# Layer norms of the token tower: five small operations moved to one visit of POOL, with new instruction orders

## What is computed

```
x = embed[tokens] + pos                                     # D = 128
for i in range(2):                                          # the "token tower"
    x = x + scan_attn(ln(x, eps=1e-6))                      # q, k, v; causal convolution of k and v; gates; 8 heads
    x = x + gelu(ln(x, eps=1e-6) @ ff1 + b1) @ ff2 + b2
h = ln(x, eps=1e-6) @ out_k + out_b                         # 256 columns
h = h + linear_attention(layernorm(h, eps=1e-5))            # no softmax, 16 heads of 64
h = h + (silu(n @ wg.T) * (n @ wu.T)) @ wd.T,  n = layernorm(h, eps=1e-5)
```

## Time and profile before

| | us |
|---|---|
| median of 3 runs | 1989.66 |
| lowest, highest | 1988.47, 1992.6 |
| the profiled execution, its own time | 1988.27 |
| its span, first to last instruction | 1986.1 |
| TensorE busy | 1850.2 |
| VectorE, ScalarE, POOL busy | 1165.6, 733.4, 439.4 |
| mean granted clock of TensorE | 0.982 of full speed |

### The profile page before, as it was taken

How to read it: one execution, slowest core, us unless ns; L and a number is a source line. 1 busy time by engine, 2 the same in 40 slices (tenths; PEclk the granted TensorE clock), 3 DMA queues, 4 the chain that set the end, 5 groups by cost and what they waited for, 6 DMA issues and landing times.

```text
span 1986.1 us, 41766 instructions
## 1 busy us (share of the span) xinstructions
PE 1850.2 (93%) x17146; PEld 1588.0 (80%) x17146; DVE 1165.6 (59%) x3019; ACT 733.4 (37%) x1444; POOL 439.4 (22%) x391
## 2 busy tenths in 40 slices
PE   4799999999999999969899999999999999999998
PEld 3678888888888888758688888888888888888887
DVE  2668888888888888755554344434444444444443
ACT  1334444554455555334323322232233223322332
POOL 3233223333222222111121122112211221122112
PEclk8899999999999999989899999999999999999999
DMA  3000000000000000022000000000000000000000
GB/s 94 5 12 18 18 17 18 16 19 16 18 17 16 15 5 9 18 86 80 17 22 1 22 22 22 1 22 22 22 1 22 22 22 1 22 22 22 1 22 22
DMA packets 29211, 42.38 MB, mean 21 GB/s; under 512 B 5856, under 2 KB 22624, under 8 KB 29024
## 3 DMA queue, kind: packets, MB, share of 16 engines
q1 hardware_dynamic: 23648, 33.49, 5.1%
q0 software_dynamic: 2048, 4.20, 0.8%
q10 hardware_dynamic: 3328, 2.04, 0.4%
HBM read 22.93 MB, written 16.78 MB: 20 GB/s over the span
## 4 chain that ended last, share of the span: by engine, by line
PE 73%; DVE 17%; issue 4%; DMA 3%; POOL 2%; ACT 1%; SPq 1%; another core or an unknown queue 0%; DVEq 0%; POOLq 0%; ACTq 0%
PE ps L1406 11%; PE ps L1407 10%; PE ps L1408 10%; PE ps L806 3%; PE ps L1008 3%; PE ps L1456 3%; PE ps L1472 3%; DVE bxn L1271 3%; PE ps L887 3%; PE ps L807 3%; PE ps L808 3%; PE ps L959 3%; PE ps L937 2%; DVE bstats L1255 2%; DMA h<-h_rows 2%
## 5 line engine op out<-in xcount | busy, mean ns | idle before, releaser
L1245 POOL TENSOR_TENSOR hids_low<-hid,hids_high 128x512 fp32r<-128x512 f32 x96 | 137.6, 1440 | 611.0 <-ACT hids_high L1392 611.0
L512 POOL TENSOR_TENSOR rstd<-var,minus_half 128x4 f32<-128x4 f32 x80 | 82.5, 1032 | 564.5 <-DVE var L599 564.4
L757 ACT ACTIVATE xn<-x,shift,rstd 128x128 f32<-128x128 f32 x320 | 130.3, 482 | 133.6 <-DVE shift L604 133.6
L676 DVE TENSOR_TENSOR att<-ps,causal 128x512 f32<-128x512 f32 x256 | 158.6, 681 | 18.1 <-PE ps L937 18.0
L1406 PE MATMUL ps<-r_high,wq_high 128*128 128x256 f32 x512 | 147.4, 288 | 0.7 <-issue 0.7
L1407 PE MATMUL ps<-r_low,wq_high 128*128 128x256 f32 x512 | 144.9, 283 | 0.0
L1408 PE MATMUL ps<-r_high,wq_low 128*128 128x256 f32 x512 | 144.8, 283 | 0.0
L1386 ACT ACTIVATE silu<-ps 128x512 f32<-128x512 f32 x96 | 57.4, 598 | 226.5 <-DVE hid L1321 159.9
L1008 PE MATMUL ps<-w_f,wide 128*128 128x128 f32 x1024 | 130.1, 278 | 0.2 <-ACT wide L801 0.2
L1008 PEld LDWEIGHTS ps<-w_f,wide 128*128 128x128 f32 x1024 | 120.8, 192 | 6.0 <-issue 5.0
L1308 DVE TENSOR_TENSOR m_low<-ps,m_high 128x512 fp32r<-128x512 f32 x32 | 22.1, 692 | 170.8 <-ACT m_high L1378 170.8
(11 more groups left out here) (352 smaller groups left out, 5060.9 us busy)
## 6 DMA issues: line engine op xcount, KB each, us to landing
h_rows<-h_out SPq DMA_DIRECT2D x16, 512.0 KB, 2.8
h<-h_rows SPq DMA_DIRECT2D x16, 512.0 KB, 3.8
out<-bxn SPq DMA_DIRECT2D x32, 256.0 KB, 2.6
taps<-in_filters ACTq DMA_DIRECT2D x1, 1024.0 KB
emb<-in_embed,idx POOLq DMA_INDIRECT x64
wk<-in_W_kT SPq DMA_DIRECT2D x1, 1024.0 KB, 6.6
stage<-in_W_vT SPq DMA_DIRECT2D x2, 512.0 KB, 6.6
stage<-in_W_q SPq DMA_DIRECT2D x2, 512.0 KB, 5.6
```

The lines of the kernel that those rows point to most:

```text
L512: pool.tensor_tensor(rstd[s][:], var[s][:], minus_half[:], ALU.pow)\
L676: dve.tensor_tensor(masked[:, :, PAIR * g:PAIR * g + PAIR, :], bank("qk", s, l, j, g, t)[:].rearrange("p (n r t) -> p n r t", n=2, r=PAIR) ...
L757: act.activation(xn[s][:, j, :], x[s][:, j, :], ACT.Identity, bias=shift[s][:, j:j + 1], scale=rstd[s][:, j:j + 1]).then_inc(xn_made[s].se ...
L1245: pool.tensor_tensor(hids[1][:, halves, :], hid[:, half, :], hids[0][:, halves, :].bitcast(F32), ALU.subtract).then_inc(hid_low[s].sem, 1)
```

## The change

The constant add moves from VectorE's `stats` to POOL, and -mean x `rstd` is done there in two steps: POOL makes `var` and -mean, then the power, then the product, in one visit. The step `shift` is gone, its order entries too. The signals are counted anew: `ln_step` rises by two a norm, `ln_rstd` by four, and `xn` waits for the fourth. The norms of the second half (`b_stats`, `b_pow`) keep their code.

```diff
@@ token_tower
-    ln_step = signals("ln_step", 4 * LN)
-    ln_rstd = signals("ln_rstd", LN)
+    ln_step = signals("ln_step", 2 * LN)
+    ln_rstd = signals("ln_rstd", 4 * LN)
@@ gpsimd
         elif step == "pow":
-            pool.wait_ge(ln_step[s].sem, ln_step[s].at(t, 4 * l + 3))
-            pool.tensor_tensor(rstd[s][:], var[s][:], minus_half[:], ALU.pow)\
-                .then_inc(ln_rstd[s].sem, 1)
+            g = ln_rstd[s]
+            pool.wait_ge(ln_step[s].sem, ln_step[s].at(t, 2 * l + 2))
+            pool.tensor_scalar(var[s][:], mv[s][:, :, 1], EPS_LN, None, ALU.add).then_inc(g.sem, 1)
+            pool.tensor_scalar(shift[s][:], mv[s][:, :, 0], -1.0, None, ALU.mult).then_inc(g.sem, 1)
+            pool.wait_ge(g.sem, g.at(t, 4 * l + 2))
+            pool.tensor_tensor(rstd[s][:], var[s][:], minus_half[:], ALU.pow).then_inc(g.sem, 1)
+            pool.wait_ge(g.sem, g.at(t, 4 * l + 3))
+            pool.tensor_tensor(shift[s][:], shift[s][:], rstd[s][:], ALU.mult).then_inc(g.sem, 1)
@@ vector
-            dve.wait_ge(g.sem, g.at(t, 4 * l + 1))
+            dve.wait_ge(g.sem, g.at(t, 2 * l + 1))
             dve.sem_inc(passed)
             for j in range(J):
                 ins = dve.bn_aggr(mv[s][:, j, :], stats[s][:, j, :])
             ins.then_inc(g.sem, 1)
-            dve.wait_ge(g.sem, g.at(t, 4 * l + 2))
-            dve.tensor_scalar(var[s][:], mv[s][:, :, 1], EPS_LN, None, ALU.add)\
-                .then_inc(g.sem, 1)
-
-        elif step == "shift":
-            dve.wait_ge(ln_rstd[s].sem, ln_rstd[s].at(t, l + 1))
-            dve.scalar_tensor_tensor(out=shift[s][:], in0=mv[s][:, :, 0], scalar=-1.0, in1=rstd[s][:],
-                                     op0=ALU.mult, op1=ALU.mult).then_inc(ln_step[s].sem, 1)
@@ scalar
         elif step == "xn":
-            act.wait_ge(ln_step[s].sem, ln_step[s].at(t, 4 * l + 4))
+            act.wait_ge(ln_rstd[s].sem, ln_rstd[s].at(t, 4 * l + 4))
```

More of the change, by code:

```diff
@@ new lines @@
+STARTS_B = [18546, 19803, 21057, 22305, 23562, 24810, 26063, 27318, 28568, 29825, 31081, 32335, 33590, 34837, 36092,
+            37347]
+PREPARE = [("w_load", 0, 17086), ("w_high", 0, 18400), ("w_low", 0, 18418), ("w_load", 1, 17230),
+           ("w_high", 1, 18894), ("w_low", 1, 19003), ("w_load", 2, 17841), ("w_high", 2, 19352),
+           ("w_low", 2, 19320), ("w_load", 3, 18736), ("w_high", 3, 19402), ("w_low", 3, 19493),
+           ("w_load", 4, 19263), ("w_scale", 4, 19621), ("w_high", 4, 19664), ("w_low", 4, 19649),
+           ("w_load", 5, 19617), ("w_scale", 5, 19648), ("w_high", 5, 19823), ("w_low", 5, 19689),
+           ("w_load", 6, 20311), ("w_scale", 6, 19673), ("w_high", 6, 19844), ("w_low", 6, 19924),
+           ("w_load", 7, 20647), ("w_scale", 7, 20185), ("w_high", 7, 20283), ("w_low", 7, 20312),
+           ("w_load", 8, 20673), ("w_scale", 8, 20248), ("w_high", 8, 20301), ("w_low", 8, 20819),
+           ("w_load", 9, 20915), ("w_scale", 9, 20410), ("w_high", 9, 20641), ("w_low", 9, 20895),
+           ("wk_load", 0, 19084), ("wo_load", 0, 18968)]
@@ new lines @@
+START_UP = [("first", 0, -6518), ("first", 1, 1550), ("first", 2, 1471), ("first", 3, 2246), ("kv_rows", 0, -7379),
+            ("kv_bias", 0, -6040), ("kv_scale", 0, -7249), ("kv_high", 0, -7358), ("kv_add", 0, -3917),
+            ("kv_low", 0, -2957), ("q_bias", 0, -5908), ("q_scale", 0, 1417), ("q_high", 0, 1512),
+            ("q_add", 0, 1185), ("q_parts", 0, 1421), ("q_low", 0, 1472), ("gate_spread", 0, 1390),
+            ("f1_bias", 0, 1665), ("f1_scale", 0, 1660), ("f1_high", 0, 2176), ("f1_add", 0, 1813),
+            ("f1_low", 0, 2111), ("head_rows", 0, 1407), ("head_bias", 0, 1859), ("head_scale", 0, 2084),
+            ("head_high", 0, 3631), ("head_add", 0, 1923), ("head_low", 0, 3714)]
```

144 lines of the change are left out of this document (62 added, 82 removed).

## The result

The changed kernel is slower: 2003.05 us in the median of its runs beside 1991.89 us for the kernel before on the same chip, ratio 1.0066 with a 95% interval of 1.0054 to 1.0079. The forecast was 1964 us, the range 1951 to 1987: both wrong, and on the wrong side.

The account below looks back on a forecast made before the run. TensorE was taken to bound the kernel, with VectorE's small operations and the norm's chain holding it up. From 1988.3 us, 15.4 (tower) and 9.8 (second half) came off: 1963.1, forecast as 1964 us, range 1951 to 1987.

Parts of the forecast that it names:

- What bounds the kernel: Tower: TensorE, 93% busy, is held up by VectorE's small operations, which POOL stretches; 2.45 us idle a group.
- `embed` in layer 0: Tower, layer 0: moving `embed` towards `state_low00` leaves 0.5 of 1.46 us waiting; gain taken as 0.9 us a group.
- The bound of 0.98 us: Tower, layer 0: the most that `state_low00`'s squaring (L664) can lose beside POOL, 1.18 - 0.19 us.
- the three operations added to POOL: Tower norms: three 128x4 operations a norm, costed at nothing because the chain to `xn` keeps its length.
- The sign I had named for it: Tower norms: a wait of `turn20` for `xn20` would show the upper end of the added operations' cost.
- my range of -0.1 to +1.8: Tower norms: cost in us a norm of the longer POOL visit if its cover is gone.
- POOL's small operation: Tower, POOL: each 128x4 operation takes 0.17 us, between 0.10 and 0.72, making a visit some 1.5 us.
- `bias00` out of layer 1: Tower, layer 1: `bias00` no longer meets `state_low10`, so TensorE's wait of 0.61 us at L951 goes.
- the new tail: Tower, group end: `f211` and `f213` become late waiting for `gelu11` and `gelu13`; 0.4 us a group taken, from 0 to 1.5.
- The second half: Attention and MLP: `b_turn`'s wait of 11.9 us goes, `m_low` costs 0.15 us a group, `gram` stays; gain 9.8 us.
- Rival 3: Tower: POOL's additions meet `state_low` in both layers and its small operations hold VectorE; 2007 us, chance 0.12.
- 0.80 for faster: Whole kernel: summed chance of a time more than 0.2%, 4 us, below the kernel before.

Follow-up runs that it names:

- pow_padded: order_only with three useless operations added behind the power in POOL's visit for layer 1's second norm: 1958.09 us, ratio 0.9884 to the kernel before.
- after_pad: The changed kernel with one idle POOL operation added behind the visit ahead of `bias00`: 1960.09 us, ratio 0.9895 to the kernel before.
- hold_embed: The changed kernel with one wait added, holding POOL's `embed` until layer 1's preceding `state_low` of the group before is done: 1970.81 us, ratio 0.9943.
- pad_one: pow_padded with one idle POOL operation in place of three: 1988.28 us, ratio 1.0036 to the kernel before.
- order_only: The code of the kernel before (`var` and `shift` on VectorE) with all orders of the changed kernel: 1985.77 us, ratio 1.0015 to the kernel before.
- second_switch: The changed kernel with two second-half steps put back, `m00` behind `keys11` and `r01` behind `b_turn00`: 1989.93 us, ratio 1.0036 to the kernel before.
- after_pad2_switch: after_pad with two idle operations in place of one, plus the two steps put back in second_switch: 1957.79 us, ratio 0.9889 to the kernel before.
- pow_padded_switch: pow_padded plus the two second-half steps put back as in second_switch: 1951.04 us, ratio 0.9847 to the kernel before.
- code_only: The code of the change with all orders of the kernel before, without the step `shift`: 1983.04 us, ratio 1.000 to the kernel before.
- bias_early: The changed kernel with `bias00` moved ahead of POOL's visit for layer 1's second norm: 1968.55 us, ratio 0.9931 to the kernel before.

## Why the prediction was wrong

**What bounds the kernel** was read rightly: TensorE, held up by VectorE's small operations, stretched in turn by POOL. In pow_padded, with the stretch nearly gone, the period is 50.97 - 48.72 = 2.25 us shorter, of 2.45 us idle a group.

**The step that failed** is the one for `embed` in layer 0: "In layer 0, `embed` moves behind `bias00` and one gather ... and towards `state_low00`, whose L664 can lose 1.18 - 0.19 = 0.98 us", "Of the 0.67 + 0.79 = 1.46 us of layer 0 I leave 0.5 us". The trace shows 2.42 us left, not 0.5. Three things were wrong in it:

- The bound of 0.98 us was the longest stretch in the trace of before, where one addition at a time met the floor. In the new order `embed` and `bias30` follow each other without a gap, and VectorE waited for both: 1.41 + 1.25 us. The bound had to be read off the new order (the sum of the additions in a row), not off the old durations.
- I costed the three operations added to POOL at nothing and said that the chain from mean and variance to `xn` keeps its length. It does not: from the power's visit to `xn20` it is 2.07 us in place of 1.38 (after_pad beside pow_padded). The sign I had named for it, `turn20` waiting for `xn20`, is hidden in the change and is there once the stall is gone: 0.68 us a group in after_pad, 1.16 in hold_embed, inside my range of -0.1 to +1.8. And the three operations push all that POOL does behind them, and by that they choose whom `bias00` and `embed` meet. pad_one, order_only and pow_padded show that this choice is worth up to 1.5% with the same work and the same order.
- The gain and the loss were summed as if independent. VectorE comes to the floor earlier because the gate steps are free, and that is how it comes in time to be caught.

**The clock** had no term at all. Before, no wait for `state` was longer than 0.8 us, the tower's clock was 1.00, and I let the price of a stall be its length. After nine of eleven stalls of 2.42 us TensorE ran at half clock. By the distances of the stalls that is 52.51 - 50.70 = 1.8 us a group, some two fifths of the 4.2 us that the collision cost.

**POOL's small operation**: 0.17 us taken, 0.24, 0.23 and 0.20 measured, with gaps of 0.07 us or so between them. A visit is 1.94 us (447.65 to 449.59), not 1.5: what was added is 0.90 us where I had 0.51. The single operation lay inside the bounds of 0.10 and 0.72 us. The power held nothing, in the changed kernel neither.

**`bias00` out of layer 1** was right: the 0.61 us at 427.03 are gone but for one wait of 0.39 us at 488.02. So, for `f211` and `f213`, was the new tail: no row for L1004 waiting for ScalarE in the change, and 2.9 us in 12 waits in hold_embed, 0.2 us a group where I had taken 0.4; `turn20`, which I had costed at nothing, came on top. Undisturbed, the orders are worth more than the 1.1 us a group I had for them.

**The second half**: `b_turn`'s wait fell from 11.9 to 4.3 us and `gram`'s stayed at 13.7, nearly as predicted. What I left out is that steps of TensorE had changed places (`m00` with `keys11`, `r01` with `b_turn00`). I costed order changes by the waits they make or mend; this one makes no wait of a matmul that a row names, and costs 0.56 us a group, 6 us by the ratios and 9 by the period over 16 groups, most of the predicted gain of 9.8. But the gain itself was not there either: with the two moves undone the period is 66.25 us, 0.17 us under the kernel before where I had taken 0.70. What `b_turn` won (7.6 us in 14 groups) the weight loads of second_switch give back waiting for `hids_low` (4.4 us) and `m_low` (2.8 us, where I had taken 2.1), rows that the kernel before does not have.

**Rival 3** ("The port", 2007 us, a chance of 0.12) was the nearest: its sign of L664 above 1.1 us is there (1232 ns), and its time. Its mechanism was half right: the additions hold the floor, in layer 0 alone and for 2.6 us; the small operations hold nothing that a row shows. Of the section "Who interferes with whom" in the Trainium skill's page "SBUF — State Buffer" I weighed one sentence in the prediction, and another mattered more: that the order of issue decides which of the two engines blocks. The traces agree for VectorE: with `embed` already running it waits (441.71, 442.98), with `embed` 0.30 us behind the floor it does not wait for `embed` (471.60, 471.90). In order_only POOL waits in its turn: a gather recorded 0.09 us behind the start of `gk` (485.14) takes 1.50 us in place of 1.10, while `gk` keeps its 0.69. That `embed` was blocked by a floor no run here shows.

**The chances**: 0.80 for faster rested on summing small terms, each read from a pair of neighbouring rows, though the timeline already showed POOL and VectorE meeting within tenths of a microsecond. A kernel whose stalls are such meetings can come out on either side of the kernel before for a shift of 0.3 us: the change and after_pad stand 1.7% apart. The rival that the train lands on the floor should have had a chance near that of the forecast.

## What to carry to other kernels

Where two engines exclude each other, lay the new order of both on one time axis: for each short operation on the critical path, ask what the other engine starts in the half microsecond ahead of it, and count the whole run of operations behind that start. Tie the loser with a wait (hold_embed) rather than leave the order to tenths of a microsecond, and look what the held engine then does late (`pow20`, 1.16 us at `turn20`); an idle operation can win more (pow_padded), but its gain hangs on one length and can be gone with the next edit. When a stall is taken away, look inside the groups of matmuls as well as at the rows of idle time: a wait that it hid can stand there. One long stall costs more than several short ones of the same sum, since the clock may fall behind it: look at the granted clock by stage before summing waits.

## What the runs showed of the hardware that was not expected

- When VectorE's floor operation waits for POOL, it ends 0.04 to 0.07 us behind the recorded end of the POOL operation that it waited for. That holds for the issue of an indirect DMA as well as for an addition: 0.40 us in after_pad and 0.72 us in after_pad2_switch are the rest of the gather's issue.
- Whether it is let in between two POOL operations that follow each other differs. L660 of the change ends at 454.80, past the end of `embed` at 453.53 and with the end of `bias30` at 454.73. In after_pad a floor that begins at 672.23, inside `embed`, ends at 672.77, just behind `embed` (672.73), though `bias30` starts at 672.67. In the runs looked at, a floor recorded at least 0.29 us ahead of the next addition went ahead of it (pow_padded, pow_padded_switch, after_pad, after_pad2_switch); one recorded 0.03 to 0.24 us ahead waited for it too (the change, code_only, bias_early, pad_one), but for two at the end of the change's tower (714.92 and 763.12, 0.09 us ahead, 0.19 and 0.20 us long). Two floors in after_pad2_switch (678.43 and 726.81) ran in 0.20 and 0.19 us while `embed` was on POOL; the first began 0.07 us ahead of the second of its two instructions (678.50). Why these four were not held stays open.
- It goes the other way as well: in order_only eleven gathers that start 0.09 us behind `gk` take 1.49 or 1.50 us, where one without such a neighbour takes 1.0 to 1.1.
- POOL's power of 1.04 us did not hold VectorE's two-input operations in these rows: L641 takes 0.19 us inside it before, L640 0.19 us in the change (448.40, the power from 448.28).
- After an idle time of 2.42 us TensorE's granted clock was 0.50 for four to seven us in nine of eleven cases; in bias_early, with waits of 1.2 us at most, in none. Shorter waits can do it: in code_only one of eight waits of 1.5 to 1.6 us was followed by such an episode (213.74), in order_only one of 1.14 us for `gk` (688.09). pad_one, with a wait of 0.60 and one of 1.19 us some three us apart, had three between 100 and 800 us.
